# Graph-attention layer on one core: loads of x chained, second unit's edges moved ahead, inverses of a batch moved behind statistics

## The chip, the cores and the metric

The kernel runs on one core of one Trainium2 chip. The metric is the device time in microseconds (us). Before the change it is 804.83 us, the median of 3 runs (804.77 to 805.94).

## The reference, cut to what matters

x has 8192 rows of 128 values, adj is an 8192 x 8192 matrix of int32 zeros and ones.

```
h   = maximum(layernorm(x), 0)
Wh  = h @ W                                   # 8192 x 128
f1, f2 = Wh @ a[:128], Wh @ a[128:]
e   = leaky_relu(f1[:, None] + f2[None, :], 0.2)
e   = where(adj == 0, -inf, e)
out = x + softmax(e, axis=1) @ Wh
```

## The kernel before, in words

The 8192 rows are taken as 16 groups of 512. Each group of output rows (q, 16 of them) needs the products with all 16 blocks of 512 neighbours (b, the "units"): 256 units in all. Everything that has to be made once, namely the normalised x, Wh, the exponentials and the pairs of 16-bit halves of them that the products read, is made for group g while the first group of output rows (q = 0) goes through its units. Only this beginning, to about 90 us, is touched by the change.

For one unit of q = 0, in the order of the data:

- The edges. A DMA from GpSimd's queue turns int32 into bytes on the way (`load_part`, L223 to L226, 256 KB written each; semaphore `first_loaded[u]`). ScalarE multiplies half of the edges by 200 (`second`, L612 to L621). GpSimd adds the two halves (`mix`, L237 to L247). TensorE transposes them (`transposes`, L390 to L397), and ScalarE unpacks them into bytes in `marks` (`unpack`, L595 to L602).
- The features. VectorE makes mean and variance (`statistics`, L782 to L795). ScalarE makes a first reciprocal root of a batch of groups (`root`, L652 to L665), and VectorE refines it (`inverses`, L797 to L815), which ends in `ln_ready`. ScalarE and GpSimd then normalise (L545 and L249), TensorE transposes and multiplies with W (`x_transposes`, `features`), ScalarE keeps Wh and takes exponentials, GpSimd scales (`scaled`, L275), ScalarE and VectorE make the two halves (`high_part` L646, `low_part` L846), which ends in `pair_ready`.
- The weights and products. VectorE makes four tiles of weights for each unit from `marks` (L860), and TensorE multiplies them with the pairs (L405 and L409).

The batches of groups are 0-1, 2-3, 4-5, 6-7, 8-11 and 12-15. The dictionary `ROOTS` says behind which unit's work the root of a batch stands: 2 (groups 4-5) at unit 0, 3 (groups 6-7) at unit 1, 4 at unit 4, 5 at unit 8. `STATS` says which groups get their statistics behind which unit; those of groups 9 and 10 stand behind the weights of unit 3, in pass b = 2 of the loop.

The order on each engine is written out by hand; each engine does its list in that order, and semaphores join the lists. x is loaded from SyncE's queue in six DMAs, `LOADS`, called x0 to x5 here: groups 0, 1, 2-3, 4-5, 6-9 and 10-15. x0, x1 and x2 are asked for at once, x3 when the first part of the edges has landed, x4 after the second and x5 after the fourth part (L189 to L194). In the loop over units VectorE's `first_weights(b + 1)` makes the weights of the next unit, with `inverses` between its two halves where `ROOTS` has the unit before (L875); unit 0 is an exception, whose `inverses` stand behind all weights (L911).

Of the kernel before, what the change touches and what calls it, by code (L numbers as in the profile page):

```python
# [59 lines left out]
def gat_kernel(nc, x, adj, W, a, out):  # L60
# [23 lines left out]
    ROOTS = {0: 2, 1: 3, 4: 4, 8: 5}  # L84
# [10 lines left out]
    with ExitStack() as ctx:  # L95
# [86 lines left out]
        @block.sync  # L182
        def _(sp):
            def load_x(k):
                lo, hi = LOADS[k]
                sp.dma_start(xm[:, lo:hi, :], x_dram[:, lo:hi, :]).then_inc(x_loaded[k], 16)


            load_x(0)  # L189
            load_x(1)  # L190
            load_x(2)
            for k, part in ((3, 0), (4, 1), (5, 3)):
                sp.wait_ge(first_loaded[part], 16)
                load_x(k)  # L194

            with sp.Fori(0, NQ - 1) as q:
                sp.wait_ge(s["rows_done"], (q + 1) * PACK)
                sp.dma_start(out_dram[:, q, :], xm[:, q, :]).then_inc(s["out_stored"], 16)
            sp.wait_ge(s["flag_ready"], 1)
            fast = sp.value_load(flag[0:1, 0:1], min_val=0, max_val=1)  # L200
            for r in range(PACK):
                sp.wait_ge(s["rows_done"], NB - PACK + r + 1)
                sl = slice(r * P, (r + 1) * P)
                sp.dma_start(out_dram[:, NQ - 1, sl], xm[:, NQ - 1, sl]).then_inc(s["out_stored"], 16)
            sp.wait_ge(s["out_stored"], 16 * (NQ - 1 + PACK))
            with sp.If(fast):
                pass
            with sp.Else():
                sp.dma_start(xm[:], x_dram).then_inc(s["x_again"], 16)
                with sp.Fori(0, NQ) as q:  # L210
                    sp.wait_ge(s["rows_done"], NB + (q + 1) * PACK)
                    sp.dma_start(out_dram[:, q, :], xm[:, q, :]).then_inc(s["out_stored"], 16)
                sp.wait_ge(s["out_stored"], 16 * (2 * NQ - 1 + PACK))
# [3 lines left out]
        def _(pool):  # L217
# [19 lines left out]
            def mix(u):  # L237

                c, k = u // KC % NC, u % KC
                if u < UN:  # L240
                    pool.wait_ge(first_loaded[u], 16)
                elif k == 0:
                    pool.wait_ge(adj_loaded[c], u // UN * 16)
                pool.wait_ge(s["second_ready"], u + 1)
                sl = slice(k * P, (k + 1) * P)
                nc.gpsimd.tensor_tensor(edges4[:, c, 0, :, sl], edges4[:, c, 0, :, sl], edges4[:, c, 1, :, sl],  # L246
                                        ALU.add).then_inc(s["mixed"], 1)  # L247

            def normalise(g):  # L249

                pool.wait_ge(s["ln_ready"], batch_of(g))
                pool.wait_ge(s["xt_ready"], g - 1)
                for r in range(1, PACK):
                    t = g * PACK + r
                    ins = nc.gpsimd.tensor_scalar(xn[:, g % 2, r * P:(r + 1) * P], xm[:, g, r * P:(r + 1) * P],  # L255
                                                  small[:, 5, t:t + 1], small[:, 6, t:t + 1], ALU.mult, ALU.add)
                ins.then_inc(s["xn_pool"], 1)
# [39 lines left out]
            mix(0)  # L297
            scaled(0)
            normalise(2)
            normalise(3)  # L300
            mix(1)
            scaled(1)
            load_part(EARLY)
            load_part(EARLY + 1)
# [238 lines left out]
        def _(act):  # L543

            def normalise(g):  # L545

                act.wait_ge(s["ln_ready"], batch_of(g))
                act.wait_ge(s["xt_ready"], g - 1)
                t = g * PACK
                nc.scalar.activation(xn[:, g % 2, 0:P], xm[:, g, 0:P], ACT.Identity, scale=small[:, 5, t:t + 1],  # L550
                                     bias=small[:, 6, t:t + 1]).then_inc(s["xn_ready"], 1)

            def relu(g):

                act.wait_ge(s["xt_ready"], g + 1)
                if g >= 2:
                    act.wait_ge(s["whp_ready"], 2 * (g - 1))
                nc.scalar.activation(ht[:, g % 2, :], stage[:, 2, :], ACT.Relu).then_inc(s["ht_ready"], 1)  # L558
# [10 lines left out]
            def keep_scaled(h):  # L569

                act.wait_ge(s["whp_ready"], 2 + h + 1)
                fresh = acc[:, 1, :] if h else stage[:, 3, :]
                for r in range(2):
                    t = PACK + 2 * h + r
                    mm = nc.scalar.activation(wh[:, t, :], fresh[:, r * 256:r * 256 + WC], ACT.Identity,
                                              scale=small[:, 5, t:t + 1])
                mm.then_inc(s["wh_ready"], 1)

            def exponentials(g):

                if g == 0:
                    act.wait_ge(s["cst_ready"], 3)
                if g == 0:
                    act.wait_ge(s["wh_first"], 2)
                else:
                    act.wait_ge(s["wh_ready"], 2 * g)
                if g >= 2:
                    act.wait_ge(s["pair_ready"], g - 1)
                sl = slice(g * PACK, (g + 1) * PACK)
                nc.scalar.activation(exps, wh[:, sl, Fo:WC], ACT.Exp, scale=1.0 - SLOPE, bias=cst[:, 0:1])  # L590
                nc.scalar.activation(tmp[:, g % 2, :, Fo:E1], wh[:, sl, E1:WC], ACT.Exp, scale=-1.0,  # L591
                                     bias=cst[:, 1:2]).then_inc(s["exps_ready"], 1)
# [19 lines left out]
            def second(q, b):  # L612

                c, k = b // KC, b % KC
                if isinstance(q, int) and q == 0:
                    act.wait_ge(first_loaded[b], 16)
                elif k == 0:
                    act.wait_ge(adj_second[c], q * 16)
                sl = slice(k * BANK // 2, (k + 1) * BANK // 2)
                nc.scalar.activation(twos[:, c, 1, :, sl], twos[:, c, 1, :, sl], ACT.Copy, scale=SECOND  # L620
                                     ).then_inc(s["second_ready"], 1)  # L621
# [30 lines left out]
            def root(k):  # L652

                sl = slice(BATCHES[k][0] * PACK, BATCHES[k][1] * PACK)
                if k == 0:
                    act.wait_ge(s["cst_ready"], 3)
                if k == 0:
                    act.wait_ge(s["mean_ready"], CENTRED)
                else:
                    act.wait_ge(s["var_ready"], k)  # L660
                nc.scalar.activation(small[:, 4, sl], stats[:, sl, 2], ACT.Ln, scale=1.0 / D, bias=cst[:, 2:3]
                                     ).then_inc(s["log_ready"], 1)
                act.wait_ge(s["log_ready"], k + 1)
                nc.scalar.activation(small[:, 3, sl], small[:, 4, sl], ACT.Exp, scale=-0.5
                                     ).then_inc(s["root_ready"], 1)  # L665
# [12 lines left out]
            root(0)  # L678
            second(0, 0)
            exponentials(0)  # L680
            relu(1)
            root(1)
            unpack(0, 0, first=True)
            high_part(0)
            normalise(2)
            keep_scaled(0)
            keep_scaled(1)
            exponentials(1)
            second(0, 1)
            relu(2)  # L690
            unpack(1, 1, first=True)
            normalise(3)
            for b in range(UN):
                if b + 1 < NQ:
                    high_part(b + 1)
# [77 lines left out]
        def _(dve):  # L773
# [90 lines left out]
            def first_weights(b):  # L864

                dve.wait_ge(s["packed_ready"], b + 1)
                if b == 0:
                    dve.wait_ge(s["rowp_ready"], 1)
                dve.wait_ge(s["marked"], b + 1)
                if b >= 2:  # L870
                    dve.wait_ge(s["used"], b - 1)
                weights(1, b, range(0, HALF))
                if b == 0:
                    low_part(b)
                elif b - 1 in ROOTS and b > 1:  # L875
                    inverses(ROOTS[b - 1])
                weights(1, b, range(HALF, PACK))
                if b > 0:
                    low_part(b)
# [27 lines left out]
            for b in range(UN):  # L907
                if b + 1 < NQ:
                    first_weights(b + 1)
                if b == 0:  # L910
                    inverses(ROOTS[b])  # L911
                    next_group(1)
                if b + 2 < NQ:
                    pack(b + 2)
                for g in STATS.get(b, ()):
                    statistics(g)

            def check():

# [124 lines left out]
```

## Time and profile before

| what | value |
|---|---|
| median of 3 runs | 804.83 us |
| the profiled execution's own time | 805.96 us |
| its span | 804.0 us |
| TensorE busy | 783.4 us, 97% |
| VectorE busy | 738.2 us, 92% |
| ScalarE busy | 482.3 us, 60% |
| GpSimd busy | 377.3 us, 47% |
| granted TensorE clock | 0.998 |
| GpSimd's DMA queue (the edges) | 67.12 MB written |
| SyncE's DMA queue (x and the output) | 8.39 MB |

The span is the time from the first to the last instruction of the profiled execution; the 1.96 us between it and that execution's own time lie around it. Times in the traces are counted from the span's start. An engine's busy time is an average over the beginning, where many short steps wait for one another, and the long rest.

### The profile page before, as it was taken

The page shows a single profiled execution, that of the slowest core. Times are in us where ns is not written, and L with a number is a line of the kernel's source. Part 1 is how long each engine was busy: PE and PEld are TensorE (multiplying, and loading weights), DVE is VectorE, ACT ScalarE, POOL GpSimd, SP SyncE. Part 2 cuts the span into 40 slices and gives each one's busy share as a digit, 9 for nine tenths or more (in the row PEclk, how much of TensorE's full clock was granted, in tenths as well). Part 3 has the DMA queues.
Part 4 walks back from the last instruction along what each step waited for, and adds up shares of the span by engine and source line. Part 5 has one row for each costly group of instructions (what it writes and reads, how often), then busy time and mean ns, then how long its engine had stood idle before and what let it go on. Part 6 is the DMA issues. An engine that isn't in the chain of part 4 may idle for free.

```text
span 804.0 us, 22478 instructions
## 1 busy us (share of the span) xinstructions
PE 783.4 (97%) x8971; PEld 719.1 (89%) x8971; DVE 738.2 (92%) x1197; ACT 482.3 (60%) x778; POOL 377.3 (47%) x501
## 2 busy tenths in 40 slices
PE   6899999999999999999999999999999999999997
PEld 5789899999999999999999999999999999999986
DVE  6998899999999999999999999999999999999996
ACT  5899855555655555565555556555555655555542
POOL 7787644543444454344445434444543444454320
PEclk9999999999999999999999999999999999999999
DMA  9999899999999999999999999999999999998200
GB/s 166 177 106 108 82 108 117 107 92 102 93 101 86 106 90 87 103 94 101 85 106 90 87 102 94 101 86 106 90 87 102 94 101 85 106 90 86 26 14 18
DMA packets 46148, 75.98 MB, mean 94 GB/s; under 512 B 2594, under 2 KB 11428, under 8 KB 46116
## 3 DMA queue, kind: packets, MB, share of 16 engines
q0 software_dynamic: 41088, 67.12, 87.9%
q1 hardware_dynamic: 4880, 8.39, 3.1%
q8 instruction: 17, 0.28, 0.1%
q14 instruction: 15, 0.12, 0.0%
q10 hardware_dynamic: 148, 0.07, 0.0%
HBM read 272.70 MB, written 4.19 MB: 344 GB/s over the span
## 4 chain that ended last, share of the span: by engine, by line
PE 91%; DVE 4%; ACT 1%; DMA 1%; issue 1%; POOL 0%; DVEq 0%; ACTq 0%; POOLq 0%
PE acc L405 54%; PE acc L409 28%; PE stage L395 7%; DVE wt_ring L860 3%; PE stage L378 1%; DMA masks<-in_adj_dram 1%; PE stage L387 1%; DVE pairs L850 1%; PE stage L360 0%; ACT marks L600 0%; ACT masks L620 0%; ACT wh L564 0%; POOL masks L246 0%; DVE stats L790 0%; DVE xm L960 0%
## 5 line engine op out<-in xcount | busy, mean ns | idle before, releaser
L860 DVE SCALAR_TENSOR_TENSOR wt_ring<-stage,packed,marks 128x512 f32<-128x512 f32 x1024 | 697.9, 744 | 51.9 <-PE acc L409 42.3
L405 PE MATMUL acc<-pairs,wt_ring 128*128 128x258 f16 x4096 | 718.7, 274 | 4.9 <-DVE pairs L850 3.9
L409 PE MATMUL acc<-pairs,wt_ring 128*128 128x129 f16 x4096 | 697.1, 219 | 0.0
L405 PEld LDWEIGHTS acc<-pairs,wt_ring 128*128 128x128 f16 x4096 | 395.9, 97 | 59.6 <-DVE pairs L850 5.4
L600 ACT ACTIVATE marks<-stage 128x1024 uint16<-128x1024 uint8 x256 | 261.9, 1023 | 291.1 <-PE stage L395 290.3
L409 PEld LDWEIGHTS acc<-pairs,wt_ring 128*128 128x128 f16 x4096 | 399.4, 98 | 2.4
L246 POOL TENSOR_TENSOR masks<-masks 128x256 int32<-128x256 int32 x256 | 184.1, 731 | 267.6 <-ACT masks L620 266.1
L620 ACT ACTIVATE masks<-masks 128x512 uint16<-128x512 uint16 x256 | 158.9, 622 | 2.3 <-DMA masks<-in_adj_dram 2.3
L262 POOL DMA_DIRECT2D masks<-in_adj_dram x120 | 87.5, 729 | 112.8 <-PE stage L395 93.4
L395 PE MATMUL stage<-ident,masks 128*128 128x128 f32 x512 | 99.2, 275 | 2.7 <-POOL masks L246 2.2
L395 PEld LDWEIGHTS stage<-ident,masks 128*128 128x128 f32 x512 | 53.1, 141 | 7.3 <-issue 3.1
L285 POOL TENSOR_SCALAR fin<-fin 128x516 f32<-128x516 f32 x15 | 22.8, 1522 | 0.5
L278 POOL TENSOR_TENSOR tmp<-wh,tmp 128x512 f32<-128x512 f32 x16 | 17.9, 1122 | 9.6 <-ACT tmp L591 9.6
L378 PE MATMUL stage<-wx,ht 128*128 128x130 f32 x120 | 20.9, 299 | 1.5 <-ACT ht L558 0.7
L637 ACT ACTIVATE fin<-acc 128x258 f32<-128x258 f32 x60 | 19.6, 388 | 3.2 <-PE acc L405 3.2
L255 POOL TENSOR_SCALAR xn<-xm,small 128x128 f32<-128x128 f32 x42 | 19.3, 468 | 4.3 <-DVE small L814 4.3
L643 ACT ACTIVATE fin<-fin,inv 128x128 f32<-128x128 f32 x60 | 19.0, 389 | 0.0
L378 PEld LDWEIGHTS stage<-wx,ht 128*128 128x128 f32 x120 | 16.6, 200 | 2.7 <-ACT ht L558 1.1
L295 POOL TENSOR_TENSOR xm<-fin,xm 128x512 f32<-128x512 f32 x15 | 17.9, 1195 | 0.3
L288 POOL TENSOR_TENSOR fin<-fin 128x516 f32<-128x516 f32 x15 | 16.5, 1102 | 1.2
L790 DVE BATCH_NORM_STATS2 stats<-xm 128x6 f32<-128x256 f32 x32 | 11.8, 420 | 3.5 <-DMA xm<-in_x_dram 3.5
L225 POOL DMA_DIRECT2D masks<-in_adj_dram x16 | 12.4, 776 | 1.0 <-POOLq L1033 0.8
(68 smaller groups left out, 144.5 us busy)
## 6 DMA issues: line engine op xcount, KB each, us to landing
masks<-in_adj_dram POOLq DMA_DIRECT2D x120, 512.0 KB, 9.0
masks<-in_adj_dram POOLq DMA_DIRECT2D x16, 256.0 KB, 22.7
out_dram<-xm SPq DMA_DIRECT2D x15, 256.0 KB, 7.5
xm<-in_x_dram SPq DMA_DIRECT2D x1, 1536.0 KB, 13.3
xm<-in_x_dram SPq DMA_DIRECT2D x2, 512.0 KB, 7.3
xm<-in_x_dram SPq DMA_DIRECT2D x1, 1024.0 KB, 10.1
xm<-in_x_dram SPq DMA_DIRECT2D x2, 256.0 KB, 3.2
out_dram<-xm SPq DMA_DIRECT2D x4, 64.0 KB, 2.2
```

Source lines behind the costliest of these rows:

```text
L246: nc.gpsimd.tensor_tensor(edges4[:, c, 0, :, sl], edges4[:, c, 0, :, sl], edges4[:, c, 1, :, sl], ALU.add).then_inc(s["mixed"], 1)
L255: ins = nc.gpsimd.tensor_scalar(xn[:, g % 2, r * P:(r + 1) * P], xm[:, g, r * P:(r + 1) * P], small[:, 5, t:t + 1], small[:, 6, t:t + 1], ...
L262: nc.gpsimd.dma_start(masks[:, at:at + HALF, :], adj_half[q, c, :, HALF * h:HALF * (h + 1), :]).then_inc(adj_second[c] if h else adj_loade ...
L285: nc.gpsimd.tensor_scalar(fin[:, :, E1:2 * E1], fin[:, :, E1:2 * E1], 1.0 / LOW, None, ALU.mult).then_inc(s["lows_scaled"], 1)
L378: mm = nc.tensor.matmul(to[:, r * 256:r * 256 + WC], ht[:, g % 2, k:k + P], wx[:], start=(r == 0), stop=(r == 1), skip_group_check=True)
L395: mm = nc.tensor.transpose(stage[:, 0, r * P:(r + 1) * P], words[:, c * PACK + r, kk * P:(kk + 1) * P], ident[:])
L405: return nc.tensor.matmul(acc[:, r, 0:2 * E1], wtv[:, w, r, 1, :], pairv[:, t, :, 0:E1], start=st, stop=end)
L409: return nc.tensor.matmul(acc[:, r, 0:E1], wtv[:, w, r, 0, :], pairv[:, t, 0, 0:E1], start=False, stop=False)
L600: nc.scalar.activation(split[:, b % MR, :].rearrange("p (s w) -> p s w", s=PACK), stage[:, 0, 0:BANK // 2].bitcast(U8).rearrange("p (w s) ...
L620: nc.scalar.activation(twos[:, c, 1, :, sl], twos[:, c, 1, :, sl], ACT.Copy, scale=SECOND).then_inc(s["second_ready"], 1)
L637: nc.scalar.activation(fin[:, r, :], acc[:, r, 0:2 * E1], ACT.Copy).then_inc(s["acc_free"], 1)
L860: nc.vector.scalar_tensor_tensor(out=wtq[:, t % NW], in0=e_row, scalar=packed[:, t, 1:2], in1=edges[:, k], op0=ALU.max, op1=ALU.mult).then ...
```

## The change

SyncE asks for x2 only when x0 has landed, and for x3 when x2 has landed, no longer when the first part of the edges has. GpSimd adds the edges of unit 1 between the two normalisings instead of behind them. ScalarE takes the root of batch 1 ahead of the relu of group 1, multiplies unit 1's edges ahead of the two copies `keep_scaled` and not behind the exponentials of group 1, and normalises group 3 ahead of unit 1's unpacking. VectorE does the inverses of batch 3 (groups 6-7) behind the statistics of group 8, no longer between the halves of unit 2's weights.

```diff
@@ sync
             load_x(0)
             load_x(1)
+            sp.wait_ge(x_loaded[0], 16)
             load_x(2)
-            for k, part in ((3, 0), (4, 1), (5, 3)):
+            sp.wait_ge(x_loaded[2], 16)
+            load_x(3)
+            for k, part in ((4, 1), (5, 3)):
                 sp.wait_ge(first_loaded[part], 16)
                 load_x(k)
@@ gpsimd
             normalise(2)
+            mix(1)
             normalise(3)
-            mix(1)
             scaled(1)
@@ scalar
             exponentials(0)
+            root(1)
             relu(1)
-            root(1)
             unpack(0, 0, first=True)
             high_part(0)
             normalise(2)
+            second(0, 1)
             keep_scaled(0)
             keep_scaled(1)
             exponentials(1)
-            second(0, 1)
             relu(2)
+            normalise(3)
             unpack(1, 1, first=True)
-            normalise(3)
@@ vector, first_weights
-                elif b - 1 in ROOTS and b > 1:
+                elif b > 2 and b - 1 in ROOTS:
                     inverses(ROOTS[b - 1])
@@ vector, the loop over units
                 for g in STATS.get(b, ()):
                     statistics(g)
+                if b == 1:
+                    inverses(ROOTS[b])
```

## Rows read from the trace of the kernel before

**Rows 1.** Stretches: length, then PE, PEld, DVE, ACT, POOL busy, clock, DMA share, GB/s.
```profile
30.00:35.00 5.00, 4.01 (x42) 3.80 (x43) 4.97 (x11) 3.45 (x10) 3.17 (x7) 1.00 1.15 215
100.00:150.00 50.00, 50.00 (x586) 46.13 (x584) 46.68 (x72) 28.83 (x44) 21.84 (x28) 1.00 1.06 111
```

**Rows 2.** The chain that ended last, from 0 us: start, length, what.
```profile
1.41 8.92 DMA masks<-in_adj_dram
```

**Rows 3.** VectorE in order of time: start, length, line, what [idle before].
```profile
9.88 0.42 DVE L832 TENSOR_TENSOR wh<-acc,small 128x260 f32<-128x260 f32 x1
...
13.88 1.41 DVE L860 SCALAR_TENSOR_TENSOR wt_ring<-stage,packed,marks 128x512 f32<-128x512 f32 x2 [0.39 <-ACT marks L600]
...
17.89 1.42 DVE L790 BATCH_NORM_STATS2 stats<-xm 128x6 f32<-128x256 f32 x4 [0.40 <-DMA xm<-in_x_dram]
19.56 2.73 DVE L860 SCALAR_TENSOR_TENSOR wt_ring<-stage,packed,marks 128x512 f32<-128x512 f32 x4 [0.24 <-ACT marks L600]
...
26.55 0.32 DVE L805 TENSOR_SCALAR small<-stats 128x8 f32<-128x8 f32 x1
27.47 0.24 DVE L807 TENSOR_TENSOR small<-small 128x8 f32<-128x8 f32 x1 [0.60 <-ACT small L664]
...
29.93 1.00 DVE L850 SCALAR_TENSOR_TENSOR pairs<-pairs,tmp 128x516 f16<-128x516 f16 x1
...
31.80 2.70 DVE L860 SCALAR_TENSOR_TENSOR wt_ring<-stage,packed,marks 128x512 f32<-128x512 f32 x4
...
35.30 1.43 DVE L790 BATCH_NORM_STATS2 stats<-xm 128x6 f32<-128x256 f32 x4
36.64 2.72 DVE L860 SCALAR_TENSOR_TENSOR wt_ring<-stage,packed,marks 128x512 f32<-128x512 f32 x4
```

**Rows 4.** ScalarE in order of time.
```profile
16.35 0.61 ACT L620 ACTIVATE masks<-masks 128x512 uint16<-128x512 uint16 x1
...
18.43 1.02 ACT L600 ACTIVATE marks<-stage 128x1024 uint16<-128x1024 uint8 x1 [0.98 <-PE stage L395]
...
28.96 0.29 ACT L591 ACTIVATE tmp<-wh,cst 128x4 f32<-128x4 f32 x1
...
42.30 0.22 ACT L664 ACTIVATE small<-small 128x16 f32<-128x16 f32 x1
```

**Rows 5.** GpSimd in order of time.
```profile
17.11 0.72 POOL L246 TENSOR_TENSOR masks<-masks 128x256 int32<-128x256 int32 x1 [0.47 <-ACT masks L620]
```

**Rows 6.** TensorE in order of time.
```profile
30.99 0.28 PE L405 MATMUL acc<-pairs,wt_ring 128*128 128x258 f16 x1 [1.65 <-DVE pairs L850]
...
45.39 0.29 PE L405 MATMUL acc<-pairs,wt_ring 128*128 128x258 f16 x1 [0.85 <-DVE pairs L850]
```

**Rows 7.** The page's part 6: x0 and x1, KB each, median us from issue to landing.
```profile
xm<-in_x_dram SPq DMA_DIRECT2D x2, 256.0 KB, 3.2
```

**Rows 8.** Line L186, x2 alone: length and start of the issue, time to landing.
```profile
L186 SPq DMA_DIRECT2D xm<-in_x_dram x1: 427/427/427, 1.8 to 1.8; - x1
...
DMA to landing us min/median/max: 7.0/7.0/7.0
```

**Rows 9.** Line L186, x3 alone: time to landing.
```profile
DMA to landing us min/median/max: 7.5/7.5/7.5
```

**Rows 10.** Line L186, x5 alone: time to landing.
```profile
DMA to landing us min/median/max: 13.3/13.3/13.3
```

**Rows 11.** Line L225, the fourth part of the edges alone.
```profile
L225 POOL DMA_DIRECT2D masks<-in_adj_dram x1: 762/762/762, 4.8 to 4.8; - x1
...
DMA to landing us min/median/max: 17.5/17.5/17.5
```

**Rows 12.** DMA queues, 13.8 to 14 us, SyncE's: packets, MB, share.
```profile
q1 hardware_dynamic: 4, 0.01, 12.0%
```

**Rows 13.** DMA queues, 14 to 15 us, GpSimd's (q0) and SyncE's (q1).
```profile
q0 software_dynamic: 112, 0.06, 66.1%
q1 hardware_dynamic: 83, 0.17, 49.6%
```

## The prediction

> **What bounds the kernel now.** I read the table by stretches first. From 100 to 150 us TensorE is busy all 50 of 50 us and VectorE 46.68 [rows 1], and so it goes on to the end: no order of the beginning makes this part shorter. The change can only alter how early TensorE comes to it. From 30 to 35 us it is the other way round: VectorE is busy 4.97 of 5 us and TensorE 4.01 [rows 1]. TensorE's list shows for what it waits there: 1.65 us for the pairs of unit 2, which end at 30.93, and 0.85 us for those of unit 5, before 45.39 [rows 6]. So up to some 60 us VectorE's list is the bound, and what counts is the idle time inside it. A gain at one place of this list lasts only if nothing further down is late for it.
>
> Next, what VectorE itself waits for [rows 3]. The first weights start at 13.88 behind a wait for `marks`. This goes back to the DMA of the first part of the edges, issued at 1.41 and landed 8.92 us later, at 10.33 [rows 2]; the other 3.5 us are multiplying, adding, transposing and unpacking. Then 0.40 us for x3 (17.89), 0.24 us for unit 1's `marks` (19.56), and 0.60 us for ScalarE's root of batch 3 (27.47). Last, the four statistics instructions of groups 9 and 10 start at 35.30 and take 1.43 us, so those of group 10, which need x5, start at about 35.30 + 0.7 = 36.0. The fourth part of the edges was issued at 4.8 and landed 17.5 later, at 22.3 [rows 11]; that releases x5, which lands 13.3 us later [rows 10], at 35.6. It is in time by 0.4 us only, and the change does not touch what releases it. This is the wait that I expect to take over.
>
> **The change part by part.**
>
> *x2 behind x0.* x0 is issued at 0.9 and takes about 3.0 to 3.2 us (median of x0 and x1, [rows 7]), so x2 is issued at about 4.0, not 1.8 [rows 8]. Before it took 7.0 us and landed at 8.8, beside the first edges. What it costs is bounded: at best the packets go out at once and share the engines evenly. Alone, SyncE's queue gets 83 packets in a us beside 112 of the edges [rows 13]; 512 KB are some 250 packets of 2 KB, so 3.1 us from about 5.1, and x2 lands at 8.2 to 9.2. At worst it has the delay of x3: issued at 10.33, when the first edges land, its first packets come in the slice from 13.8 to 14 [rows 12], 3.5 us later, and it lands 7.5 us after its issue [rows 9]. Then x2 lands at 4.0 + 7.5 = 11.5. I take 9.0, since x2's packets come up about when the edges' first do and not into a full queue. The work that hides this: `keep_scaled` of group 0 stands behind the statistics of x2 and ended at 9.88 + 0.42 = 10.3 [rows 3], but the exponentials need ScalarE, which multiplies the first edges from 10.33 on for 0.6 us. So 0.6 us of delay are free; at 9.0 the cost is nothing, at 11.5 about 1.7 to 2.0 us at the first weights. The first edges have to share with x2 for longer on most engines, but their last bytes came by engines that already shared; I leave them at 10.3, with +0.8 as a bound (150 more packets at 195 a us).
>
> The Trainium skill, "DMA: Bandwidth & Descriptors", section "Queues, rings and completion order", says that each DMA engine takes turns between its queue rows, a packet at a time. By it x2 could never be held up by the edges, and the good end would be certain. The trace disagrees in part: x3 got nothing for 3.5 us, and only then shared [rows 12, 13]. I keep the bad end as a case.
>
> *x3 behind x2.* Issued at about 9.1 and not 10.33, it lands at about 16.6 by its own 7.5 us, not 17.9. That removes the 0.40 us at 17.49. SyncE's list is in order, so x4 now stands behind two more waits; both end before the second part of the edges lets it go, and it is not late.
>
> *Unit 1's edges earlier.* Before, ScalarE multiplied them at 16.35, and GpSimd added them at 17.11 for 0.72 us [rows 4, 5]; only then, at 18, could TensorE transpose, and ScalarE sat idle 0.98 us until it could unpack at 18.43 [rows 4]. Now the multiplication stands about 1.8 us earlier (14.5), the sum at about 15.2, behind the three instructions of group 2, and TensorE is ready after its eight tile products, at 17.6. Against it: the two copies and the exponentials move back 0.5 us. The first product of k = 0 with r = 1 waits for those copies, at 16.4, so about 0.1 of the gain goes. Unpacking starts at about 18.0, and unit 1's weights at 19.1 where they were at 19.56: **-0.45** there, if x3's two statistics (1.43 us, from 17.5) are done by 18.9, as they are. The normalising of group 3 ahead of the unpacking falls into ScalarE's idle time and releases TensorE's transposes; VectorE gets nothing by it at once. root(1) first saves 0.5 us of wait in `inverses(1)`, which VectorE spends waiting for `marks` anyway: nothing.
>
> *inverses(3) behind group 8's statistics.* From 26.55 to 31.80 VectorE does inverses(3), half of unit 2's weights, its low part, pack and one group of statistics [rows 3]: 5.25 us. The wait of 0.60 us goes. The instructions beside GpSimd's work were slow; the low part took 1.00 [rows 3] where others take 0.7. The pairs of unit 2 come at about 28.1, after the earlier -0.45, instead of 30.93, so the 1.65 us of TensorE's wait vanish for unit 2. But the pack behind them needs the exponentials of group 3, done at 28.96 + 0.29 = 29.25 [rows 4], perhaps 28.8 now: a new wait of 0.3 to 0.7 us. Net **-0.75**, between 0 (the wait only changes its name) and -1.3. The `ln_ready` of groups 6 and 7 comes at about 30.6 instead of 28.6; GpSimd asks for it near 31.9, so nothing.
>
> *The sum at 36.* VectorE would come to group 10 at 36.0 - 0.45 - 0.75 = 34.8. There x5 stops it until 35.6, which only leaves 36.0 - 35.65 = **-0.35**, and 0.85 us of the gain are lost as idle time. x5 depends on the fourth part of the edges. With x2 on all engines beside the first edges and x4 as late as before I put this part between unchanged and 0.4 later, so -0.35 to +0.05; I take -0.15.
>
> *Behind it.* The root of batch 4 was ready at 42.30 + 0.22 = 42.52 [rows 4], when VectorE was at 42.14 to 42.6 and had some 0.25 us of waiting in it. ScalarE hangs there on TensorE's features of groups 4 to 6, which now come 1.5 us earlier because unit 2 does. So **-0.25**. The pairs of unit 5 come 0.4 earlier, TensorE goes on from there, and the whole rest shifts.
>
> Sum: -0.15 - 0.25 = -0.4 us. On the profiled execution: 805.96 - 0.4 = 805.56 (span 803.6). That execution stands 1.1 us over the median of 804.83, so by the median **804.4 us**.
>
> **The rivals.**
>
> *A, the forecast:* x5 is the new wait. 804.4. For it: 0.4 us of slack against 1.2 us of gain ahead of it. Against: the landing can move by itself.
>
> *B, all of it comes through:* x5 lands a us earlier, or the early queue makes the fourth part of the edges earlier. Then -1.2 - 0.25 = -1.45, and 803.4; with the whole -1.3 of the inverses 802.8.
>
> *C, x2 behind the edges' packets:* it lands at 11.5 and the first weights are 1.7 us later, unit 1's 1.3 later (20.9). With -0.75 at unit 2 VectorE comes to group 10 at 36.0 + 1.3 - 0.75 = 36.5, +0.5, less 0.25: 805.1. In its favour are x3's 3.5 us. The Trainium skill ("DMA: Bandwidth & Descriptors", section "Rules for kernel authors") wants a load asked for early and waited for late; holding x2 back is the opposite.
>
> *D, the slower one: x5 lands late.* Place: group 10's statistics. x3 now shares with the edges from about 12.6 on, and shared edges advance at 112 packets a us [rows 13] instead of some 195. If the fourth part so lands 1.4 us later, at 23.7, x5 lands at 37.0, and VectorE, which was there at 36.0, is 1.05 later; less 0.25 is +0.8: 805.6. It decides from a landing of x5 at 36.2 on (36.0 plus the 0.25 behind it).
>
> **How the numbers follow.** About 0.2% (1.6 us: under 803.2 or over 806.4) is what a measurement can tell from no change. A 0.55, B 0.16, C 0.16, D 0.13. Faster: half of B, where the full size of the inverses is needed, and a little of A for its sizes: 0.13. Slower: only C and D in an extreme (both together are 804.4 + 1.9): 0.08. Within: 0.79. The range goes from B's better part, 803.2, to D with some room, 805.9.
>
> **What would show it.** Right: x2 lands at 8.5 to 9.3; x3 before 17.4 and no wait at 17.9; unit 1's weights at about 19.1; the first product of unit 2 without a wait near 29; VectorE idle some 0.8 us ahead of group 10 until x5 lands at 35.6 to 36.0, named as a DMA of x; unit 5's first product at about 45.0. Wrong: no wait for x at 35 (B, then unit 5 starts at 44.2 or before); x2 landing after 10.5 and first weights after 15 (C); x5 after 36.2 (D); or a wait at 60 us and later that I took for shifting along.

## The result, and the profile after

The changed kernel takes 809.79 us (median of 5 runs, 808.83 to 810.50) beside 804.83 us before (5 runs, 804.54 to 805.94): ratio 1.0056, 95% interval 1.0041 to 1.0071. It is slower by 0.6%; the forecast was 804.4 and its range ended at 805.9. The profiled execution took 809.33 us with a span of 807.4, 3.4 us more than before's span. Of all executions below one, of e12, was a slow one (1359.06 us at a granted clock of 0.56), and e12's ratio is taken without it.

The chain that ended last (start, length, what), its beginning in the changed kernel:

```profile
0.87 3.02 DMA xm<-in_x_dram
3.90 8.77 DMA xm<-in_x_dram
...
12.77 0.76 DVE stats L793 x2
13.53 0.66 DVE wh L835 x2
...
15.24 1.12 PE stage L390 x4
...
20.97 1.03 ACT marks L603
...
22.09 2.73 DVE wt_ring L863 x4
```

Before, it began with the edges [rows 2]; now it begins with x0 and then x2. x2 is asked for at 3.9 and takes 8.8 us. Line L186's own view, from 3 to 8 us, and the packets (queue: packets, MB, share; q0 is GpSimd's queue, q1 SyncE's) in three stretches, 3.8 to 4, 4.2 to 7.7 and 7.7 to 8 us. Of the first only q0's line is shown; what q1 moves there is the rest of x1:

```profile
L186 SPq DMA_DIRECT2D xm<-in_x_dram x1: 395/395/395, 3.9 to 3.9; - x1
...
  DVE stats L793: 4.2, 1
...
DMA to landing us min/median/max: 8.8/8.8/8.8
```

```profile
q0 software_dynamic: 4, 0.00, 15.0%
```

```profile
q0 software_dynamic: 522, 0.26, 105.5%
```

```profile
q0 software_dynamic: 42, 0.02, 98.9%
q1 hardware_dynamic: 5, 0.01, 10.0%
```

The edges' first packets come before 4, when x0 has landed and x1 is nearly through. In the kernel before, the first one came only at 5.1 to 5.2, with x2's packets ahead of it (GpSimd's queue in that slice):

```profile
q0 software_dynamic: 1, 0.00, 6.0%
```

In the changed kernel nothing of x moves at all from 4.2 to 7.7 us; x2's first packet comes 3.8 us after x2 was asked for. VectorE (start, length, what, idle time before) waits for it:

```profile
12.77 0.76 DVE L793 BATCH_NORM_STATS2 stats<-xm 128x6 f32<-128x256 f32 x2 [4.17 <-DMA xm<-in_x_dram]
...
13.77 0.42 DVE L835 TENSOR_TENSOR wh<-acc,small 128x260 f32<-128x260 f32 x1
...
16.98 1.41 DVE L863 SCALAR_TENSOR_TENSOR wt_ring<-stage,packed,marks 128x512 f32<-128x512 f32 x2 [0.38 <-ACT marks L603]
...
20.51 1.42 DVE L793 BATCH_NORM_STATS2 stats<-xm 128x6 f32<-128x256 f32 x4
22.09 2.73 DVE L863 SCALAR_TENSOR_TENSOR wt_ring<-stage,packed,marks 128x512 f32<-128x512 f32 x4 [0.16 <-ACT marks L603]
...
31.81 0.17 DVE L844 TENSOR_SCALAR packed<-stage 128x8 f16<-128x8 f32 x1 [0.60 <-ACT tmp L594]
...
33.10 0.61 DVE L811 SCALAR_TENSOR_TENSOR small<-small 128x8 f32<-128x8 f32 x1
...
33.95 0.58 DVE L817 SCALAR_TENSOR_TENSOR small<-stats,small 128x8 f32<-128x8 f32 x1
34.46 2.71 DVE L863 SCALAR_TENSOR_TENSOR wt_ring<-stage,packed,marks 128x512 f32<-128x512 f32 x4
...
39.30 2.72 DVE L863 SCALAR_TENSOR_TENSOR wt_ring<-stage,packed,marks 128x512 f32<-128x512 f32 x4
41.92 1.50 DVE L853 SCALAR_TENSOR_TENSOR pairs<-pairs,tmp 128x516 f16<-128x516 f16 x1
```

These lines answer to [rows 3]: first weights 16.98 for 13.88 (+3.1), unit 1's 22.09 for 19.56 (+2.5), unit 3's 34.46 for 31.80 (+2.7), unit 4's 39.30 for 36.64 (+2.7). ScalarE had multiplied the first edges a us earlier than before, and then stood 4.4 us for group 0's `keep_scaled`, which stands behind x2 in VectorE's list:

```profile
9.28 0.63 ACT L623 ACTIVATE masks<-masks 128x512 uint16<-128x512 uint16 x1 [1.27 <-DMA masks<-in_adj_dram]
14.29 0.27 ACT L593 ACTIVATE stage<-wh,cst 128x8 f32<-128x8 f32 x1 [4.38 <-DVE wh L835]
...
15.34 0.58 ACT L561 ACTIVATE ht<-stage 128x512 f32<-128x512 f32 x1
15.82 1.02 ACT L603 ACTIVATE marks<-stage 128x1024 uint16<-128x1024 uint8 x1
```

### The profile page after: what moved, and what is told of

Its sections match the earlier page's. It is cut to its first block, busy times and chain, and to the rows that moved or that the text cites. A ratio compares the mean times of both kernels' runs of the same rounds, so it can differ in the third digit from the quotient of the medians.

```text
span 807.4 us, 22478 instructions
## 1 busy us (share of the span) xinstructions
PE 784.1 (97%) x8971; PEld 718.7 (89%) x8971; DVE 738.8 (92%) x1197; ACT 482.6 (60%) x778; POOL 377.3 (47%) x501
## 4 chain that ended last, share of the span: by engine, by line
PE 91%; DVE 5%; DMA 1%; ACT 1%; issue 1%; POOL 0%; ACTq 0%; DVEq 0%; POOLq 0%
PE acc L408 54%; PE acc L412 28%; PE stage L398 7%; DVE wt_ring L863 3%; DMA xm<-in_x_dram 1%; PE stage L381 1%; PE stage L390 1%; DVE pairs L853 1%; DVE stats L793 1%; PE stage L363 1%; ACT marks L603 0%; ACT wh L567 0%; DVE xm L965 0%; DVE small L811 0%; ACT pairs L652 0%
## 5 line engine op out<-in xcount | busy, mean ns | idle before, releaser
L863 DVE SCALAR_TENSOR_TENSOR wt_ring<-stage,packed,marks 128x512 f32<-128x512 f32 x1024 | 697.9, 744 | 51.8 <-PE acc L412 42.3
L265 POOL DMA_DIRECT2D masks<-in_adj_dram x120 | 87.5, 729 | 112.8 <-PE stage L398 93.3
L281 POOL TENSOR_TENSOR tmp<-wh,tmp 128x512 f32<-128x512 f32 x16 | 17.9, 1122 | 12.7 <-ACT tmp L594 12.7
L258 POOL TENSOR_SCALAR xn<-xm,small 128x128 f32<-128x128 f32 x42 | 18.8, 457 | 6.3 <-DVE small L817 6.1
L567 ACT ACTIVATE wh<-stage 128x260 f32<-128x260 f32 x28 | 10.7, 382 | 4.7 <-PE stage L381 4.6
```

The lines of the kernel that those rows point to most:

```text
L265: nc.gpsimd.dma_start(masks[:, at:at + HALF, :], adj_half[q, c, :, HALF * h:HALF * (h + 1), :]).then_inc(adj_second[c] if h else adj_loade ...
L863: nc.vector.scalar_tensor_tensor(out=wtq[:, t % NW], in0=e_row, scalar=packed[:, t, 1:2], in1=edges[:, k], op0=ALU.max, op1=ALU.mult).then ...
```

## The experiments

All were timed beside the kernel before on the same chip, 5 runs each where the loss is large and 10 to 12 in the others. The columns in the middle are from each one's profiled execution, in us: when x2 landed, and when the weights of units 0, 1, 4 and 6 start. Then come the median and the ratio to before.

| kernel | what it is | x2 | unit 0 | unit 1 | unit 4 | unit 6 | us | ratio (95%) |
|---|---|---|---|---|---|---|---|---|
| before |  | 8.8 | 13.88 | 19.56 | 36.64 | 46.20 | 804.83 | |
| changed | the whole change | 12.7 | 16.98 | 22.09 | 39.30 | 49.37 | 809.79 | 1.0056 (1.0041-1.0071) |
| e1 | only the new loads of x | 12.4 | 16.44 | 22.36 | 39.45 | 49.00 | 809.10 | 1.0044 (1.0030-1.0058) |
| e2 | changed, old loads of x | 6.1 | 13.06 | 18.16 | 35.37 | 45.43 | 805.81 | 1.0007 (0.9998-1.0016) |
| e3 | changed, only x3 behind x2 | 6.4 | 13.15 | 18.25 | 35.46 | 45.52 | 805.88 | 1.0005 (0.9996-1.0014) |
| e4 | only the inverses moved | 8.7 | 13.73 | 19.25 | 36.47 | 46.52 | 806.18 | 1.0008 (0.9999-1.0017) |
| e5 | e4, low part between | 6.6 | 12.84 | 18.40 | 35.62 | 44.80 | 804.92 | 0.9996 (0.9987-1.0005) |
| e6 | e2, low part between | 6.4 | 13.09 | 18.19 | 35.40 | 44.59 | 804.42 | 0.9994 (0.9985-1.0003) |
| e7 | e1, group 0 ahead of x2 | 12.5 | 15.58 | 21.66 | 38.76 | 48.31 | 808.39 | 1.0040 (1.0026-1.0054) |
| e8 | changed, x2 asked for at 3.4 | 11.9 | 16.20 | 21.46 | 38.67 | 48.73 | 809.36 | 1.0051 (1.0037-1.0065) |
| e9 | changed, edges behind x0 | 7.4 | 15.79 | 21.61 | 40.15 | 50.57 | 808.77 | 1.0044 (1.0031-1.0057) |
| e10 | e6, inverses ahead of the pack | 8.3 | 13.47 | 18.98 | 35.12 | 44.37 | 804.15 | 0.9986 (0.9978-0.9995) |
| e11 | e10, x5 one part earlier | 6.7 | 13.08 | 18.40 | 35.65 | 45.20 | 804.76 | 0.9996 (0.9988-1.0005) |
| e12 | only ScalarE and GpSimd | 5.9 | 13.11 | 18.72 | 35.79 | 45.37 | 804.88 | 0.9996 (0.9987-1.0005) |

The medians of before on the other chips were 805.31 (e1 to e4), 805.45 (e5 to e8) and 805.12 (e9 to e12). Two things have to be known to read the profile columns. First, where x2 is asked for at once, it lands at 5.9 to 6.7 in some profiled executions and at 8.3 to 8.8 in others. The first part of the edges goes with it, landing at 9.1 to 9.5 or at 9.9 to 10.4, and so do the first weights, at 12.8 to 13.2 or at 13.5 to 13.9. So gains between units are compared as distances within one execution.

Second, TensorE is slower at the beginning, and until when differs between executions. The same transposition of x takes 421 ns until 15.7 us in before and until 18.8 us in the changed kernel, then 273 ns; in e4 it takes 273 ns at 15.1 us already. The distance from unit 0 to unit 1 moves with it a little: it is 5.68 us in before, and 5.52 and 5.56 in e4 and e5, which have the same orders up to there. And in two kernels that hold x2 back the granted clock fell once more. These are their rows of stretches (as in [rows 1]), the first two of e7, the last two of e9. In the second row of each pair TensorE had 0.50 of the clock, the lower of its two levels (1.2 and 2.4 GHz); in the row before it, it was busy 2.65 of 6.8 and 2.00 of 4 us:

```profile
11.50:18.30 6.80, 2.65 (x25) 2.22 (x24) 4.98 (x14) 4.26 (x12) 3.28 (x7) 1.00 1.20 149
18.40:21.70 3.30, 2.97 (x17) 2.34 (x15) 2.34 (x8) 1.66 (x4) 3.20 (x5) 0.50 1.14 238
35.00:39.00 4.00, 2.00 (x24) 1.64 (x22) 3.97 (x8) 2.83 (x7) 3.98 (x7) 0.99 1.24 106
39.00:42.30 3.30, 3.30 (x20) 2.98 (x18) 3.30 (x8) 1.35 (x3) 1.76 (x4) 0.50 1.24 105
```

### e1: only the loads of x

```diff
             load_x(1)
+            sp.wait_ge(x_loaded[0], 16)
             load_x(2)
-            for k, part in ((3, 0), (4, 1), (5, 3)):
+            sp.wait_ge(x_loaded[2], 16)
+            load_x(3)
+            for k, part in ((4, 1), (5, 3)):
```

> Only the loads of x as changed (x2 behind x0, x3 behind x2); all orders on ScalarE, GpSimd and VectorE as before. Theory Q (x2, asked for when the edges' packets are already queued, comes behind them, and VectorE stands at group 2's statistics): x2 lands at 12 to 13 us, the first weights start at about 16.5 to 17.0 instead of 13.88, and nearly the whole loss is here: 2.5 to 3.5 us over before. Theory O (the loss comes from the new orders, above all the root of batch 1 ahead of the relu, and the inverses of batch 3 later): under 1 us over before.

Measured 1.0044. x2 lands at 12.4, and VectorE's list has the same hole:

```profile
12.46 0.76 DVE L793 BATCH_NORM_STATS2 stats<-xm 128x6 f32<-128x256 f32 x2 [3.79 <-DMA xm<-in_x_dram]
...
16.44 0.75 DVE L863 SCALAR_TENSOR_TENSOR wt_ring<-stage,packed,marks 128x512 f32<-128x512 f32 x1
```

By this the loss lies with the loads, as theory Q has it: the new order of x alone is 3.8 us over its own before by the medians, most of the whole loss, and a little more than the 2.5 to 3.5 expected. The reason that theory Q gives, packets already queued ahead of x2, is another matter; e8 tests it.

### e2 and e3: all but the order of x; and with x3 alone behind x2

e2 is the changed kernel with the old loads of x. e3 has this in their place:

```diff
             load_x(1)
             load_x(2)
+            sp.wait_ge(x_loaded[2], 16)
+            load_x(3)
-            for k, part in ((3, 0), (4, 1), (5, 3)):
+            for k, part in ((4, 1), (5, 3)):
```

> The whole change without the new order of x. Theory Q: x2 lands at 8.8 as before, the first weights start at 13.9, unit 1's at about 19.1, and VectorE meets the landing of x5 at 35.6; 0 to 0.6 us faster than before. Theory O: 1 us or more slower than before, and the first weights later than 13.9.

> The whole change, but x2 is asked for at once as before; x3 still waits for x2's landing alone. Theory Q: only holding back x2 costs; x3 asked for at 8.8 lands at about 16.3, the first weights are at 13.9, the time is within 0.5 us of the kernel that keeps the old order of x. Rival: x3 sharing with the edges from 12.3 us on is what pushes the parts of the edges and x5 back; then x5 lands a us or more later than 35.6 and the time is 1 us over the kernel with the old order of x.

Both can't be told from before (1.0007, 1.0005) nor from each other. The loss is gone: holding back x2 costs, letting x3 follow x2 does not (x3 lands at 14.3 in e3; x5 at 33.4, not later). But the small gain expected of e2 is not there either. Its distances tell why: unit 0 to 1 takes 5.10 us (before 5.68), 1 to 4 17.21 (17.08), 4 to 6 10.06 (9.56). The first gains 0.58 and the others lose 0.63. Not all of the 0.58 is the change's: before's execution had x3 late as well, 0.40 us [rows 3]. e5 and e6 below differ only in the orders on ScalarE and GpSimd, and both have x3 at 16.3 to 16.4; there the distance is 5.56 and 5.10, so these orders give 0.46.

### e12 and e4: the new orders one by one

e12 has only the new orders on ScalarE and GpSimd, e4 only the moved inverses, as in the diff of the change.

> Only the new orders on ScalarE and GpSimd; loads of x and VectorE's inverses as before. By the forecast unit 1's weights start 0.45 us earlier after the first weights (5.2 instead of 5.68 us behind them), which carries to the end: 0.2 to 0.6 us faster than before. Rival (VectorE's wait for the root of batch 3 at unit 2 takes it back): unit 3's weights 0 to 0.1 us earlier than before relative to the first weights, and the same time as before.

> Only the inverses of batch 3 (groups 6 and 7) behind the statistics of group 8; everything else as before. As forecast: 0.75 us gained on VectorE at unit 3's weights (31.1 instead of 31.8), of which the landing of x5 at 35.6 leaves 0.35, and 0.25 behind it: 0.3 to 0.6 us faster. Rival (the wait only changes its name, from ScalarE's root to the exponentials of group 3, as the changed kernel's trace suggests, where unit 3's weights stood 2.66 later and unit 2's 2.53): no gain at unit 3, 0 to 0.2 us slower or faster.

e12: 0.9996, no difference. Unit 0 to 1 takes 5.61, because x3 landed at 17.34 and held group 4's statistics; in e2, where x3 landed at 16.3, the same orders gave 5.10. VectorE in e12:

```profile
17.36 1.43 DVE L790 BATCH_NORM_STATS2 stats<-xm 128x6 f32<-128x256 f32 x4 [0.64 <-DMA xm<-in_x_dram]
```

From unit 1 on e12 keeps before's distances (17.07, 9.58), its 0.61 us of waiting for the root of batch 3 with them. So the rival's result came, but by the landing of x3 first. e4: 1.0008, and its interval just reaches no change; a gain of 0.3 to 0.6 us is ruled out. Here unit 1 to 4 takes 17.22: the 0.60 us of waiting went from ScalarE's root to the exponentials of group 3, as the rival said, and the moved inverses themselves are slow (33.10 and 33.95 in the changed kernel, 0.6 us each). And unit 4 to 6 takes 10.05 for 9.56, which nobody had forecast. e4's VectorE and GpSimd at unit 4's low part:

```profile
39.09 1.49 DVE L850 SCALAR_TENSOR_TENSOR pairs<-pairs,tmp 128x516 f16<-128x516 f16 x1
```

```profile
38.98 1.05 POOL L278 TENSOR_TENSOR tmp<-wh,tmp 128x512 f32<-128x512 f32 x1 [1.26 <-ACT tmp L591]
```

The low part takes 1.49 us and ends 0.55 us after GpSimd's multiplication, at 40.58.

### e5 and e6: unit 4's low part between its weights

e5 is e4, e6 is e2, each with:

```diff
                 weights(1, b, range(0, HALF))
-                if b == 0:
+                if b in (0, 4):
                     low_part(b)
 ...
                 weights(1, b, range(HALF, PACK))
-                if b > 0:
+                if b not in (0, 4):
                     low_part(b)
```

> The inverses moved as in the change, and in addition the low part of unit 4 stands between the halves of unit 4's weights and not behind them; everything else as before. Theory P (VectorE's low part, with 16-bit output, is held up while a two-input addition or multiplication of GpSimd runs: 1.49 us at unit 4 where GpSimd scales at the same time, 0.7 elsewhere): moved by 1.3 us it meets no such work and takes 0.7; unit 5's weights start 0.8 us earlier than in the kernel with only the inverses moved (40.7 instead of 41.45), and the time is 0.5 to 0.9 us below that kernel. Rival (the 1.49 us come from ScalarE or TensorE being behind, or belong to unit 4's data): the low part stays above 1.2 us and the time is the same.

> The whole change without the new order of x, with unit 4's low part between the halves of its weights. Theory P: 0.6 to 0.9 us below the same kernel with the low part behind the weights, thus 0.2 to 1.0 us faster than before, at most about 2 us where x2 lands early. Rival (the landing of x5 at 35.6 takes the gain): VectorE waits for x5 and the time equals before's.

Theory P holds. In e5 the low part takes 0.69 us, before GpSimd's multiplication starts:

```profile
36.92 0.69 DVE L850 SCALAR_TENSOR_TENSOR pairs<-pairs,tmp 128x516 f16<-128x516 f16 x1
```

```profile
38.13 1.05 POOL L278 TENSOR_TENSOR tmp<-wh,tmp 128x512 f32<-128x512 f32 x1 [1.26 <-ACT tmp L591]
```

Unit 4 to 6 takes 9.18 and 9.19 us for 10.05 and 10.06, 0.87 less in both pairs. By the ratios e5 is 0.12% under e4 and e6 0.13% under e2, about a us each. The intervals of each pair overlap, so it is the profiles that carry this. Neither can be told from before.

### e7: who stands behind x2

As e1, and on VectorE:

```diff
-            statistics(2)
             keep_scaled(0)
             keep_scaled(1)
-            statistics(3)
             pack(0)
+            statistics(2)
+            statistics(3)
             inverses(1)
```

> Only the loads of x as changed, but VectorE scales and keeps group 0 and packs it ahead of group 2's statistics, so that these steps don't stand behind x2. Theory Q with VectorE's list as the carrier: x2 lands at 12 to 13 us as in the kernel with only the loads changed, and the first weights start at about 15.5 instead of 16.4; 0.5 to 1.0 us below that kernel, still 2.5 us over before, since the root and inverses of batch 1 stand behind x2 too. Rival (the first weights wait for the edges or for group 2's data whatever VectorE does): no change against the kernel with only the loads changed.

As expected in the profile: first weights at 15.58 for 16.44 with x2 as late as in e1, and unit 6 still 0.7 us earlier. So 0.7 to 0.9 us of the loss is that group 0's steps stand in the list behind the wait for x2; the rest stayed, with the inverses of batch 1, which need x2, still ahead of the first weights. The time, 808.39 us, can't confirm it: its ratio is only 0.0004 under e1's, and the intervals overlap.

### e8 and e9: what the delay depends on

e8 is the changed kernel with x2 behind GpSimd's clearing of the identity:

```diff
             load_x(1)
-            sp.wait_ge(x_loaded[0], 16)
+            sp.wait_ge(s["ident_zero"], 1)
             load_x(2)
```

> The whole change, but x2 is asked for when GpSimd has cleared the identity (3.3 to 3.4 us) and not when x0 has landed (3.9 us). The edges' first packets came at 3.9 us in the changed kernel and at 5.1 us before it. Theory Q, a queue that fills: x2 still comes behind the edges' packets but meets a shorter queue, its first packets come before 7.9 us and it lands between 8.5 and 11.5, and the time lies between before and the changed kernel, 1 to 3 us over before. Rival (a fixed delay of some 4 us for any load asked for while the edges move): x2 lands at 12.0 to 12.5 and the time is within 0.7 us of the changed kernel's.

Here my theory lost to its rival: asked for 0.5 us earlier, x2 gets its first packet 3.8 us later again, just after 7.1, and lands 8.5 us after its issue. Line L186 from 3 to 8 us, then GpSimd's packets from 3.3 to 3.9 and SyncE's from 7.1 to 7.3:

```profile
L186 SPq DMA_DIRECT2D xm<-in_x_dram x1: 395/395/395, 3.4 to 3.4; - x1
...
DMA to landing us min/median/max: 8.5/8.5/8.5
```

```profile
q0 software_dynamic: 1, 0.00, 3.4%
```

```profile
q1 hardware_dynamic: 3, 0.01, 9.0%
```

x2 was even asked for half a us ahead of the edges' first packet, the single one before 3.9. So it is no queue that fills with time but a near-constant delay: 3.5 to 3.8 us from issue to first packet. In the fourteen traces 30 of the loads x2 to x5 have a first packet that stands apart from the load ahead of them, and 29 show this delay; the thirtieth is x2 in e9, below. It fits this too that before's x2, asked for at 1.8 with its packets ahead of the edges' first at 5.1, was not held up.

e9 is the changed kernel with the edges asked for behind x0 too:

```diff
-            load_part(0)
-            load_part(1)
             nc.gpsimd.memset(ident[:], 0.0).then_inc(s["ident_zero"], 1)
 ...
-            for u in range(2, EARLY):
+            pool.wait_ge(x_loaded[0], 16)
+            for u in range(0, EARLY):
                 load_part(u)
```

> The whole change, and in addition GpSimd asks for all parts of the edges only when x0 has landed, so that x2, asked for at the same 3.9 us, meets no packets of the edges. Fixed delay only beside the edges (x2, x3, x5 got their first packet 3.6 to 3.8 us after they were asked for while the edges moved, x0 1.0 us in a quiet queue): x2's first packets come at about 5.0 and it lands at 6.2 to 6.8; the first part of the edges lands at about 11.5, the first weights start at about 15.0 instead of 16.98, and the time is 1.5 to 2.5 us below the changed kernel although everything is asked for later. Rival (the delay belongs to an ask that follows a wait, whatever else moves): x2 still lands after 11 and the time is the changed kernel's or over it.

x2 is asked for at 3.8, behind the same wait, and gets its first packets a us later; it lands 3.6 us after its issue. The edges' first packet comes at 6.7. Line L186 from 3 to 5 us, the packets from 4.8 to 5, and ScalarE's list:

```profile
L186 SPq DMA_DIRECT2D xm<-in_x_dram x1: 396/396/396, 3.8 to 3.8; - x1
...
DMA to landing us min/median/max: 3.6/3.6/3.6
```

```profile
q1 hardware_dynamic: 8, 0.02, 102.0%
```

```profile
12.27 0.63 ACT L622 ACTIVATE masks<-masks 128x512 uint16<-128x512 uint16 x1 [4.18 <-DMA masks<-in_adj_dram]
...
17.15 0.63 ACT L622 ACTIVATE masks<-masks 128x512 uint16<-128x512 uint16 x1 [0.60 <-DMA masks<-in_adj_dram]
```

So the delay comes with the edges' traffic and not with the wait. The same execution has both cases: x3, asked for at 7.4 after the edges have started, gets its first packet only after 11, 3.6 us later. The time I had wrong: 808.77, about a us below the changed kernel by the medians (the intervals overlap) and not 1.5 to 2.5. The edges are late instead, the first part at 12.25 and the second at 17.13, and ScalarE waits 4.18 and 0.60 us for them; x4, asked for behind the second part, lands at 27.4 and holds VectorE's statistics for 1.41 us. Its units 4 and 6 in the table may stand too late for the kernel: the profiled execution was its longest (810.52 us) and has the stretch at half the clock from 39.0 to 42.3.

### e10 and e11: a better version, and the gate that I had forecast

e10 is e6 with the inverses ahead of the pack; e11 also asks for x5 one part of the edges earlier:

```diff
+                if b == 1:
+                    inverses(ROOTS[b])
                 if b + 2 < NQ:
                     pack(b + 2)
                 for g in STATS.get(b, ()):
                     statistics(g)
-                if b == 1:
-                    inverses(ROOTS[b])
```

```diff
-            for k, part in ((3, 0), (4, 1), (5, 3)):
+            for k, part in ((3, 0), (4, 1), (5, 2)):
```

> The new orders without the new order of x, unit 4's low part between the halves, and the inverses of batch 3 ahead of the pack of group 3, in the 0.6 us in which VectorE waited for the exponentials. They took 1.5 us behind group 8's statistics (two of the five beside GpSimd's work, 0.6 each). Expected: unit 3's weights at 29.5 to 29.9 instead of 30.56, and then the old forecast's gate is tested: if x5 lands at 33.7 or before (as in the runs where x2 landed before 7), VectorE gets through at 33.6 to 34 and the time is 0.7 to 1.2 us below that kernel, 1.5 to 2 us below before; in executions where x5 lands at 35.6, VectorE waits for it at group 10's statistics and the gain is 0 to 0.4. Rival: the inverses meet GpSimd's work here too and the gain at unit 3 is under 0.3.

> As the kernel with the inverses ahead of the pack, and x5 asked for when the third part of the edges has landed, not the fourth. If x5 gates VectorE at group 10's statistics: x5 lands earlier by up to 3 us and the time falls by 0.3 to 1 us more. Rival (x5 is no gate, or its earlier packets push the fifth to seventh parts of the edges back, which ScalarE then waits for): the same time or 0.5 us more.

e10 takes 804.15 us, ratio 0.9986 (0.9978 to 0.9995), the only one whose interval lies under before. The gain, about a us, is less than the 1.5 to 2 expected for a landing of x5 at 33.7 or before (it was 34.4), and under the 0.2% that the prediction took for what a measurement can tell; its size is not to be leaned on. VectorE in e10:

```profile
28.02 0.16 DVE L805 TENSOR_SCALAR small<-stats 128x8 f32<-128x8 f32 x1
...
28.70 0.17 DVE L814 SCALAR_TENSOR_TENSOR small<-stats,small 128x8 f32<-128x8 f32 x1
...
29.74 2.71 DVE L860 SCALAR_TENSOR_TENSOR wt_ring<-stage,packed,marks 128x512 f32<-128x512 f32 x4
...
33.24 0.76 DVE L790 BATCH_NORM_STATS2 stats<-xm 128x6 f32<-128x256 f32 x2
34.44 0.77 DVE L790 BATCH_NORM_STATS2 stats<-xm 128x6 f32<-128x256 f32 x2 [0.43 <-DMA xm<-in_x_dram]
35.12 1.40 DVE L860 SCALAR_TENSOR_TENSOR wt_ring<-stage,packed,marks 128x512 f32<-128x512 f32 x2
```

The five steps of the inverses now take 0.8 us and fill the wait, and unit 1 to 3 takes 10.76 us for 12.24 before. And here x5, landed at 34.41, stops group 10's statistics for 0.43 us. In e11 x5 lands at 31.7, and it is of no use, as the rival said: the sixth part of the edges lands at 32.05 (29.5 in e10) and ScalarE, then VectorE, wait for it:

```profile
32.08 0.63 ACT L620 ACTIVATE masks<-masks 128x512 uint16<-128x512 uint16 x1 [1.59 <-DMA masks<-in_adj_dram]
```

```profile
34.03 0.17 DVE L841 TENSOR_SCALAR packed<-stage 128x8 f16<-128x8 f32 x1 [1.29 <-ACT tmp L591]
```

## Why the prediction was wrong, point by point

- **What bounds the kernel**: right. What the beginning loses arrives at the end: first weights +3.1, unit 6 +3.2, span +3.4 us.
- **x2 behind x0**: the step that failed. I took a landing at 9.0, at no cost, and let 11.5 be the worst; it was 12.7, and 11.9 to 12.7 in all four kernels that hold x2 back and not the edges. The price of a late landing was right: 1.7 to 2.0 us at 11.5 makes 2.9 to 3.2 at 12.7, and 3.1 was measured. For the landing, two things were wrong. I let the edges' first packets start at 5.1 whatever x2 does; with x2 away they start at 3.8, ahead of it. And I took a full queue for the condition of x3's delay, where e8 showed the same 3.8 us in the first moments. The rows told more than I took from them: x3 got nothing for 3.5 us [rows 12], and so did x5 (3.6 us), which I had not looked up. The worst case took all of x3's 7.5 us over, 3.6 to the first packet and 3.9 from there to the landing; for x2 it was 3.8 and 5.0. Why its packets took a us longer is open.
- **Rival C** had the mechanism and not the size. It gave +1.7 at the first weights (measured +3.1), and the gains that it set against this were not there: 805.1, measured 809.8.
- **x3 behind x2**: in the change x3 was asked for at 12.7, not 9.1, and landed at 20.2; harmless by e3 where x2 is early.
- **Unit 1's edges earlier, -0.45**: right in size, -0.46 from e5 to e6; but nothing where x3 holds the statistics (e12).
- **inverses(3), -0.75**: wrong. Distance unit 1 to 4 rose by 0.14 (e4). I had seen the new wait and put it at 0.3 to 0.7 us, but held the instructions' stretching for a thing of their old place; they meet GpSimd's work in the new one too (0.61 and 0.58 us), and unit 4's low part fell upon GpSimd's multiplication (+0.5 to unit 6). The term "behind it", -0.25, had the wrong sign by this.
- **x5 as the new wait**: not in the changed kernel, where x5 landed at 34.3 and VectorE came at 38.6. It exists, as e10 shows, where VectorE comes to it at 34.0, 2.0 us earlier than before; in the change the gain that was to bring VectorE there did not come.

What stays open: the changed kernel's median is 5.0 us over before, its profiled execution only 3.4. Before's profiled execution was one with x2 at 8.8, and before's times lie from 804.5 to 806.6 on all chips; that the lower ones are those with x2 at 6 is likely from the profiles of e2, e3, e5, e6 and e12, and was not shown. TensorE's clock may have a part in it. In before no execution had a mean granted clock under 0.998, but 14 of the 25 of the kernels that hold x2 back (changed, e1, e7, e8, e9) had 0.994 to 0.997. The profiles of e7 and e9, each with a stretch at half the clock, have 0.996 and 0.997. In e1 and e8 the four executions at 0.995 took 809.1 to 809.9 us and the six others 808.3 to 809.4; in the changed kernel no such difference is seen. No trace shows such an execution of the changed kernel. Nor did any run show where the 3.8 us arise.

## What to carry to other kernels

Before an early load is held back for another's landing, look for what else will be moving when it is asked for: read the time from issue to first packet of a load that was asked for in such traffic, not of one in a quiet queue, and put that whole delay on every instruction that stands behind the wait in its engine's list. And when a piece of an in-order list moves, check each neighbour on the other engine for overlap in its new place; a gain of half a us is lost by one instruction that comes to lie beside the wrong work.

## What the runs showed of the hardware

- A load from SyncE's queue asked for while GpSimd's converting loads moved, or up to half a us before their first packet (e8), got its own first packet 3.5 to 3.8 us later, in 29 cases, at least one in each of the fourteen traces. It was 1.0 us later where they did not move (x0 in all, x2 in e9). The Trainium skill, "DMA: Bandwidth & Descriptors", section "Queues, rings and completion order", has the DMA engines take turns packet by packet; that is seen only after this delay.
- An instruction of VectorE with both inputs in SBUF is held up by one of GpSimd's that started just before it: the low part of unit 4 took 1.49 us and ended 0.55 us after GpSimd's multiplication, in the changed kernel, e2, e3, e4 and e8, and 0.69 us elsewhere (e5). It goes the other way too: at unit 5 of before the low part started first, at 44.61, and took 0.73 us, and GpSimd's multiplication, started at 44.76, took 1.48 us for its usual 1.05. The Trainium skill, "SBUF — State Buffer", section "SBUF: two separate sides", says that such an instruction and one of GpSimd that reads SBUF exclude one another for the whole instruction; the trace agrees with its 1.49 against 0.69 us and 1.48 against 1.05. The weights, with one input in PSUM, kept their 0.74 us (0.72 to 0.76 in all traces to 62 us).
- The granted clock of TensorE fell to 0.50 for over 3 us after stretches in which TensorE was busy 2.65 of 6.8 us (e7) and 2.00 of 4 us (e9). A mean clock of 0.997 or less stood in 14 of 25 executions that hold x2 back, in none of before's and in one of 88 of the other experiments; that the late load is the cause was not shown.
